# A graph and mixture-of-experts layer on one core: three banks for the experts' products, a thinner spread of edge batches, later edge lists

## The reference

```
all_msg = einsum('nf,rfo->rno', xn, weight)            # 16 relations
gate    = sigmoid(einsum('nf,rf->rn', xn, gate_weight))
msg     = all_msg[rel, src] * norm * gate[rel, src]    # one row per edge
x1 = x + relu(segment_sum(msg, dst)) + mix(xn)         # mix: linear attention
xn2 = layernorm(x1)
for e in range(8):                                     # top 2 of 8 experts
    h = gelu(xn2 @ w1[e] + b1[e]);  y = h @ w2[e] + b2[e]
    out = out + combine[:, e] * y                      # out starts as xn2
return x1 + out
```

## Time and profile before

| | us |
|---|---|
| median of 3 runs | 1874.82 |
| lowest, highest | 1874.43, 1874.87 |
| the profiled execution | 1876.67 |
| its span in the trace | 1874.8 |
| TensorE busy | 1744.3 (93%) |
| VectorE busy | 1266.6 (68%) |
| ScalarE busy | 943.5 (50%) |
| GpSimd busy | 817.8 (44%) |

### The profile page before, as it was taken

How to read it: one execution, slowest core, us unless ns; L and a number is a source line. 1 busy time by engine, 2 the same in 40 slices (tenths; PEclk the granted TensorE clock), 3 DMA queues, 4 the chain that set the end, 5 groups by cost and what they waited for, 6 DMA issues and landing times.

```text
span 1874.8 us, 28079 instructions
## 1 busy us (share of the span) xinstructions
PE 1744.3 (93%) x9706; PEld 1510.7 (81%) x9706; DVE 1266.6 (68%) x3596; ACT 943.5 (50%) x1845; POOL 817.8 (44%) x816
## 2 busy tenths in 40 slices
PE   5999999999999799998589999999999989999888
PEld 4887888888888688887478888888888888888878
DVE  6555555444443678887568788797787886878854
ACT  4555555555554545553245545455454453654543
POOL 2000000000000377777767666677667765667700
PEclk8999999999999999999799999999999999999999
DMA  6555777755554674444433333434334333333300
GB/s 209 219 222 214 277 292 280 273 213 213 213 213 199 221 269 148 149 154 145 133 114 100 123 115 96 135 103 121 110 102 133 117 106 107 102 120 109 109 18 17
DMA packets 124801, 295.89 MB, mean 158 GB/s; under 512 B 18522, under 2 KB 85968, under 8 KB 116596
## 3 DMA queue, kind: packets, MB, share of 16 engines
q1 hardware_dynamic: 86132, 189.63, 27.5%
q0 software_dynamic: 38528, 104.46, 18.8%
HBM read 162.70 MB, written 131.32 MB: 157 GB/s over the span
## 4 chain that ended last, share of the span: by engine, by line
PE 57%; DVE 16%; POOL 14%; issue 7%; ACT 2%; DMA 2%; SPq 1%; DVEq 0%; ACTq 0%; POOLq 0%
PE bank L49 17%; PE bank L51 16%; PE bank L50 16%; POOL msg L616 14%; PE bank L1379 3%; DVE agg L1001 3%; DVE parts L646 2%; DVE msg_low L835 2%; DMA msg<-messages,idxT 2%; DVE onehot_norm L828 1%; PE bank L1268 1%; PE bank L1375 1%; PE bank L1419 1%; DVE rest L967 1%; PE bank L1377 1%
## 5 line engine op out<-in xcount | busy, mean ns | idle before, releaser
L616 POOL DMA_INDIRECT msg<-messages,idxT x784 | 806.0, 1028 | 960.7 <-issue 841.9
L49 PE MATMUL bank<-parts 128*128 128x512 f32 (+2 forms) x2180 | 813.6, 373 | 61.6 <-DVE agg L1001 48.0
L51 PE MATMUL bank<-parts 128*128 128x512 f32 (+2 forms) x2180 | 771.2, 354 | 0.0
L50 PE MATMUL bank<-parts 128*128 128x512 f32 (+2 forms) x2180 | 769.3, 353 | 0.0
L49 PEld LDWEIGHTS bank<-parts 128*128 128x128 f32 x2180 | 419.5, 192 | 123.2 <-issue 61.3
L51 PEld LDWEIGHTS bank<-parts 128*128 128x128 f32 x2180 | 419.0, 192 | 55.0
L50 PEld LDWEIGHTS bank<-parts 128*128 128x128 f32 x2180 | 420.0, 193 | 49.0
L1092 ACT ACTIVATE plain<-bank,plain 128x256 f32<-128x256 f32 x392 | 163.7, 469 | 245.9 <-PE bank L51 243.6
L689 DVE TENSOR_SCALAR plain<-bank,plain 128x256 f32<-128x256 f32 x392 | 171.0, 478 | 165.0 <-PE bank L51 111.2
L1188 ACT ACTIVATE rest<-bank,small 128x512 f32<-128x512 f32 (+1 forms) x208 | 134.1, 662 | 252.7 <-PE bank L51 239.7
L1159 ACT ACTIVATE msg_high<-msg,nrmT 128x256 fp32r<-128x256 f32 x392 | 175.3, 500 | 124.5 <-DMA msg<-messages,idxT 119.6
(11 more groups left out here) (169 smaller groups left out, 1536.7 us busy)
## 6 DMA issues: line engine op xcount, KB each, us to landing
messages<-plain SPq DMA_DIRECT2D x49, 2048.0 KB, 7.0
xnT_scratch<-parts SPq DMA_DIRECT2D x98, 128.0 KB, 3.2
msg<-messages,idxT POOLq DMA_INDIRECT x784, 2.8
mix_parts<-xnT_scratch SPq DMA_DIRECT2D x23, 512.0 KB
parts<-xnT_scratch SPq DMA_DIRECT2D x10, 1024.0 KB, 4.8
w_parts<-piece_parts SPq DMA_DIRECT2D x32, 256.0 KB, 2.4
parts<-w_parts SPq DMA_DIRECT2D x4, 2048.0 KB, 16.8
plain<-in_x SPq DMA_DIRECT2D x48, 128.0 KB, 7.0
```

The source lines that it names most:

```text
L49: e.matmul(out, left(0), right(0), start=start, stop=False)
L50: e.matmul(out, left(0), right(1), start=False, stop=False)
L51: return e.matmul(out, left(1), right(0), start=False, stop=stop)
L616: e.indirect_dma_start(msg[:, b % SLOTS, j, :], None, table_rows, bass.IndirectOffsetOnAxis(idxT[:, j, b:b + 1], 0)).then_inc(s_gather[b % ...
```

## The change

Three things are done. The halves of the experts' products take the banks 6, 7 and 2 in turn, by a number that counts all halves. In the first group's chain a batch is placed after `fold` 1 and after every second `ready` step only; the batches left over fall to `share`. And GpSimd waits for all relation weights before it loads the edge lists, while VectorE and ScalarE take the small operands after the third block of weights, the gate sum after the fifth and the first sigmoid after the sixth.

```diff
     for i in range(3):
         order.append(("fold", i))
-        more()
+        if i == 1:
+            more()
     for i in range(READY):
         ready(0, i)
-        more()
+        if i % 2 == 1:
+            more()
...
+        def y_bank(u, p):
+            return bank[(6, 7, 2)[(2 * u + p) % 3]]
...
+            for n in range(NB):
+                e.wait_ge(s_w_in[n], 16 * KH)
             for a, t in zip((src, dst, rel, norm.rearrange("e a -> (e a)")), (src_i, dst_i, rel_i, nrm_f)):
...
                     low(lambda i: w_p[:, i, k, c], w_raw[:, k, c]).then_inc(s_w_low, 1)
-            e.wait_ge(s_turn_small, 1)
-            e.tensor_copy(small[:, 0:2 * R + 2 * X], bank[7][:, 0:2 * R + 2 * X])
...
-            sum_gates(0)
+                if n == 2:
+                    e.wait_ge(s_turn_small, 1)
+                    e.tensor_copy(small[:, 0:2 * R + 2 * X], bank[7][:, 0:2 * R + 2 * X])
...
+                if n == 4:
+                    sum_gates(0)
...
                     e.copy(w_p[:, 0, k, c], w_raw[:, k, c]).then_inc(s_w_high, 1)
-            e.wait_ge(s_small, 1)
...
-            sigmoid(0)
+                if n == 2:
+                    e.wait_ge(s_small, 1)
...
+                if n == 5:
+                    sigmoid(0)
...
             def free_y(g, x_, p):
-                u = y_use[g, x_]
-                if u:
-                    e.wait_ge(s_y_add, 2 * u + p - 1)
+                n = 2 * y_use[g, x_] + p
+                if n >= 3:
+                    e.wait_ge(s_y_add, n - 2)
...
-                            m = three(e, bank[6 + p][:, (k % 2) * D:(k % 2 + 1) * D],
+                            m = three(e, y_bank(y_use[g, x_], p)[:, (k % 2) * D:(k % 2 + 1) * D],
```

More of the change, by code:

```diff
@@ L774, in vector_program @@
                     low(lambda i: w_p[:, i, k, c], w_raw[:, k, c]).then_inc(s_w_low, 1)
-            e.wait_ge(s_turn_small, 1)
-            e.tensor_copy(small[:, 0:2 * R + 2 * X], bank[7][:, 0:2 * R + 2 * X])
-            e.tensor_copy(b1T, bank[7][:, 64:64 + KH * X]).then_inc(s_small, 1)
-            e.wait_ge(s_gate_w_high, 1)
-            low(lambda i: gate_p[:, :, i, :], gateT.rearrange("p (h r) -> p h r", h=KH)).then_inc(s_gate_w_low, 1)
-            e.wait_ge(s_route_w_high, 1)
-            low(lambda i: route_p[:, :, i, :], routerT.rearrange("p (h r) -> p h r", h=KH)).then_inc(s_route_w_low, 1)
-            e.wait_ge(s_b2_high, 1)
-            low(lambda i: b2_p[0:2 * X, i, :], b2_rows).then_inc(s_b2_low, 1)
-            e.wait_ge(s_bout_high, 1)
-            low(lambda i: bout_p[0:1, i, :], bout_row).then_inc(s_bout_low, 1)
-            sum_gates(0)
+                if n == 2:
+                    e.wait_ge(s_turn_small, 1)
+                    e.tensor_copy(small[:, 0:2 * R + 2 * X], bank[7][:, 0:2 * R + 2 * X])
+                    e.tensor_copy(b1T, bank[7][:, 64:64 + KH * X]).then_inc(s_small, 1)
+                    e.wait_ge(s_gate_w_high, 1)
+                    low(lambda i: gate_p[:, :, i, :], gateT.rearrange("p (h r) -> p h r", h=KH)).then_inc(s_gate_w_low, 1)
+                    e.wait_ge(s_route_w_high, 1)
+                    low(lambda i: route_p[:, :, i, :], routerT.rearrange("p (h r) -> p h r", h=KH)).then_inc(s_route_w_low, 1)
+                    e.wait_ge(s_b2_high, 1)
+                    low(lambda i: b2_p[0:2 * X, i, :], b2_rows).then_inc(s_b2_low, 1)
+                    e.wait_ge(s_bout_high, 1)
+                    low(lambda i: bout_p[0:1, i, :], bout_row).then_inc(s_bout_low, 1)
+                if n == 4:
+                    sum_gates(0)
             for t in range(TILES):
@@ L995, in y_add @@
                     for k in ks:
-                        y = bank[6 + p][:, (k % 2) * D:(k % 2 + 1) * D]
+                        y = y_bank(u, p)[:, (k % 2) * D:(k % 2 + 1) * D]
                         row = agg[:, START[g] + k, :]
@@ L1103, in scalar_program @@
                     e.copy(w_p[:, 0, k, c], w_raw[:, k, c]).then_inc(s_w_high, 1)
-            e.wait_ge(s_small, 1)
-            e.copy(gate_p[:, :, 0, :], gateT.rearrange("p (h r) -> p h r", h=KH)).then_inc(s_gate_w_high, 1)
-            e.copy(route_p[:, :, 0, :], routerT.rearrange("p (h r) -> p h r", h=KH)).then_inc(s_route_w_high, 1)
-            e.wait_ge(s_rows_in, 16 * 6)
-            e.copy(b2_p[0:2 * X, 0, :], b2_rows).then_inc(s_b2_high, 1)
-            e.copy(one_p[0:1, :], ones1[:, :])
-            e.copy(bout_p[0:1, 0, :], bout_row).then_inc(s_bout_high, 1)
-            sigmoid(0)
+                if n == 2:
+                    e.wait_ge(s_small, 1)
+                    e.copy(gate_p[:, :, 0, :], gateT.rearrange("p (h r) -> p h r", h=KH)).then_inc(s_gate_w_high, 1)
+                    e.copy(route_p[:, :, 0, :], routerT.rearrange("p (h r) -> p h r", h=KH)).then_inc(s_route_w_high, 1)
+                    e.wait_ge(s_rows_in, 16 * 6)
+                    e.copy(b2_p[0:2 * X, 0, :], b2_rows).then_inc(s_b2_high, 1)
+                    e.copy(one_p[0:1, :], ones1[:, :])
+                    e.copy(bout_p[0:1, 0, :], bout_row).then_inc(s_bout_high, 1)
+                if n == 5:
+                    sigmoid(0)
             for t in range(TILES):
@@ L1480, in bias @@
                         for i in range(2):
-                            m = e.matmul(bank[6 + p][:, (k % 2) * D:(k % 2 + 1) * D], combT[0:2 * X, k * P:(k + 1) * P],
+                            m = e.matmul(y_bank(y_use[g, X], p)[:, (k % 2) * D:(k % 2 + 1) * D], combT[0:2 * X, k * P:(k + 1) * P],
                                          b2_p[0:2 * X, i, :], start=i == 0, stop=i == 1)
```

## The result

The changed kernel takes **1863.43 us** (median of 4 runs, 1860.03 to 1863.91), the kernel before 1874.62 beside it (4 runs). The ratio is 0.9937, 95% interval 0.992 to 0.9955: 11 us faster, where the prediction said 32 and its range ended at 1863. The profiled execution of after is 1863.91 us, its span 1862.1.

A forecast was written before the change was run, and what follows sets the result against it. TensorE, busy 93% of the span, was taken as the bound, so time could be won only where it idles or runs at its lower clock. Terms -4.0 - 26.5 + 9.8 + 8 + 3 - 18 - 4.5 = -32.2 gave 1843 us, range 1822 to 1863.

The forecast's parts named there:

- Opening, -4.0: Opening: earlier small operands and later edge loads start the sixth product 5.9 us earlier, about 2 given back; 4.0 us gained.
- Rival (d): Opening: edge lists land at 36 or later, VectorE waits and the 4 us are lost; 1847, chance 0.06.
- Chain, -26.5: First group's chain: with eight batches fewer, gathers no longer set its length; 26.5 us gained, bounds 15 to 32.
- Rival (c): First group's chain: held by its loads and own latency, it gives only 12 of 26.5 us; 1857, chance 0.10.
- Eight batches, +9.8: Experts' stage: the eight moved batches cost TensorE 1.23 us each, no idle covering it; 9.8 us lost.
- Third bank, -18: Experts' stage: a third product bank shortens TensorE's waits for adds; 18 us gained, bounds 0 and 32.
- -4.5 behind: Last 75 us, without batches: the third bank shortens four waits of 7.8 us together; 4.5 us gained.
- Rival (a): Experts' stage: the third bank gives nothing, as VectorE is late for other uses too; 1865, chance 0.12.
- Heaps, +8: Before the mixes of late groups: TensorE idles at heaps of five and four batches; 8 us lost, between 0 and 14.
- denser gathers, +3: Experts' stage: denser gathers and a busier VectorE add late splits elsewhere; 3 us lost, between 0 and 10.
- Rival (e): Experts' stage: gathers become its pace; 1894 at 6.1 us a batch, chance 0.04.

The follow-up runs named there:

- halved gathers: Changed kernel with batches from 154 on fetching two of their four chunks, all else kept: 1834.4 us, ratio 0.9796.
- level deal: Changed kernel with batches dealt evenly and just in time to each of the last four groups: 1829.13 us; with the chain as before: 1835.19 us.
- barer chain: Changed kernel with batches dealt evenly and just in time to the last four groups, two batches instead of seven in the first group's chain: 1839.61 us, ratio 0.9813.

## Why the prediction was wrong, point by point

Against the kernel with opening and bank but the thick chain the loss can be placed. That kernel's span is 26.5 us shorter than before's, just what the terms of opening and bank add up to (-4.0, -18, -4.5), but by the medians of the runs it is 22, so the close hit is partly luck. The thin chain on top of it was forecast at -5.7 (-26.5 + 9.8 + 8 + 3) and measured +13.8 by the spans, 11.6 by the medians. So by the spans the whole miss, and by the medians most of it, is in what the eight moved batches do.

**Opening, -4.0: right.** The page of after has 3.9 us at the start of the keys and values. Over all profiled executions that start is at 611.2 to 613.6 with the opening and at 616.5 to 618.1 without it, 5.3 us apart on the mean. With and without it beside the bank, the ratios are 0.9888 and 0.9908, with intervals that overlap. Rival (d) did not come: L707 starts at 29.79 with no wait.

**Chain, -26.5: right in mechanism, some 4 us too large.** At the first bias product after has 25.7 (29.6 less 3.9), but part of that is the luck of one execution. From the start of the keys and values to that product take 331.4 to 335.4 us in the four kernels with the thick chain and 309.7 to 312.9 in the five with seven batches, 22.5 apart on the mean; between the kernel with opening and bank and the changed one it is 21.2. The parts of the term erred both ways. At the first expert product the chain itself gives 21.1 instead of 25.4. Of the 4.3 missing, 2.4 lie in front of the chain: its first product L1402 (L1391 in before) stands 256.7 us behind the start of the keys and values, against 254.2 in before. This stretch is 254.2 to 258.3 us in the other kernels outside B, with either chain, so it is spread and not the change. What makes it long in after is a look-ahead, too: ScalarE waits for a gather, VectorE's work for the fold stands behind it, and TensorE idles (timeline of after):

```profile
866.63 0.91 ACT L1170 ACTIVATE msg_high<-msg,nrmT 128x256 fp32r<-128x256 f32 x2 [5.97 <-DMA msg<-messages,idxT]
...
870.26 3.78 PE L1402 MATMUL bank<-rest 128*128 128x256 f32 x8 [5.69 <-DVE rest L887]
```

From the first expert product to the first bias product 4.6 us went instead of 1.1, and the two errors nearly cancel. Rival (c), 12 of 26.5, falls.

**Eight batches, +9.8: right, as the changed kernel had them.** From the kernel without the thin chain to the changed one, groups 0 to 7 went from 597.5 to 604.0, 1.3 us a batch against 1.23. With five more (109 in groups 0 to 7) each costs 2.0.

**Third bank, -18: right; -4.5 behind: three times too large.** Alone it gives 12.4 in groups 0 to 7 and 5.8 in 8 to 11, together 18.2. Behind them it gives 1.6, where 5.2 of 7.8 us of waits were expected to go. The whole kernel is 16.6 faster by the medians, against 22.5 forecast. The waits for its adds fell from 40.2 to 21.1 in the experts' stage of the changed kernel, and to 16.2 with the bank alone. In groups 0 to 7 one of 1.4 to 3.5 us is left in nearly each group. The working counted ten waits above 1.44 us, by 12.7 together; the trace has twelve, by 13.6, so 26.6 us could go and not 27.5. Rival (a) falls. The rule named beside it (the Trainium skill, TensorE: Matmul & The Clock Gate, section HAM oscillation) does not carry over: it comes from a kernel that had been slowed by waits for DMA, and 0.9908 for the bank alone decides here.

**Heaps, +8, and denser gathers, +3: wrong, and this is the step that failed.** Groups 8 to 11 took 28.3 us more than without the thin chain; 3.9 of it are three batches, so 24.4 stand against 11, outside the bound of 14 that I gave the heaps and at the far end of 24 for both terms. Three things were left out.

1. I counted what TensorE waits for at the heap's own batches (6 us forecast, 7.0 read) and took the heap as over with its last sum. The reason I gave for these waits was not the one at work either: the fifth's gather was said to start only when the first had been summed, but that sum ended at 1538.4 and the gather began at 1542.4, 0.30 us behind the gathers of the fourth. GpSimd's pace held it. What ScalarE and VectorE have behind it was not followed: their look-ahead of two batches, written down in the description of the kernel itself, puts two batches that are not yet gathered in front of the gelu's casts and splits. That is 11.2 us of TensorE's waits for L653, and with the halved gathers both waits were gone.
2. I priced idle time alone. The heaps also cost clock, 11 us over the four groups in the windows, and the level deal, which took away the waits, took away the clock's loss too. The same prediction had used just such a row for the opening, where it gave back 2 us for a half-clock stretch.
3. The heap of three in front of group 11 was said to grow and was priced at nothing; group 10, from bias to bias, lost 8.6 us against before (73.4 against 64.8), of which one more batch is 1.3.

The range missed for the same reason: its upper end took the rivals one at a time, and no rival was a heap that costs more than 14.

**Rival (e)**, gathers as the pace of the whole stage, was wrong for the changed kernel (GpSimd still waits 76.4 us for TensorE, though 50 were expected), but the barer chain shows that it is near: at 14 batches a group a batch more costs 2.0 us and not 1.2.

Why the uneven deal costs so much more with heaps of five, four and three than with three, two and two is shown only for the sum (38 against 13 us, by the level deal at either chain; 5.2 and 2.4 of them in group 11, which has no heap). I did not run one heap by itself. Nor is a shorter look-ahead tried, since the number of buffers and the order of all four engines hang on it.

## What to carry to other kernels

When work is dealt out evenly and a dependency collects what is missing, the collected heap is the price of the deal, not the average density: list the heaps first, and make the deal meet each due time. A heap costs at the engines that work ahead: follow each of them past its end to the next thing in its order that the bounding engine needs, and add the clock that the bounding engine loses behind each wait. And a stage that waits for gathers stops being worth thinning once its own chain of steps is the longer.

## What the runs showed of the hardware

In the sets called B the same programs took 6 to 9% longer, 2036 against 1874 us for the kernel before and 1984 against 1852 for the one with opening and bank. In the latter's first 600 us TensorE is busy 581 us in either. From there on, where GpSimd's gathers run, they part. Windows of the same work, from 600 to the first bias product and from there to the ninth, first outside B, then in B:

```profile
600.00:944.50 344.50, 302.04 (x1572) 256.67 (x1570) 260.61 (x658) 155.01 (x340) 238.47 (x246) 0.93 0.52 170
944.50:1541.90 597.40, 580.80 (x3641) 519.72 (x3640) 484.57 (x1434) 307.34 (x559) 418.84 (x395) 0.99 0.39 115
```
```profile
600.00:1005.40 405.40, 320.33 (x1569) 267.75 (x1567) 260.43 (x658) 153.79 (x340) 239.12 (x247) 0.88 0.44 144
1005.40:1644.60 639.20, 601.48 (x3642) 527.67 (x3641) 486.74 (x1434) 307.12 (x559) 409.56 (x394) 0.97 0.36 108
```

VectorE, ScalarE and GpSimd are busy for as long in both, within 3%; what grows is idle time, and TensorE's granted clock is lower. In B TensorE has waits for nothing that the profile names, up to 6.7 us at 980, in the first group's chain. Two lines of its waits from 944 to 1542:

```profile
PE bank L1450 <- issue: 7.1, 2, 6.7
PE bank L49 <- issue: 5.0, 8, 1.4
```

A gather takes GpSimd the same in both (1009 and 1032 ns on the mean). What stalls the engines in B is open, and so is whether it belongs to the chip. The signs for bank, chain and level deal agree in and outside B, the sizes don't: the bank gives 1.6 to 2.2% there and 0.9% here.
